# Masking the second halves' diagonal blocks after the exponential, on GpSimd, in a new order of stages

## The chip, the cores and the metric

The kernel runs on one core of a Trainium2 chip, in one launch. The metric is device microseconds of one execution, host transfers not included. Four engines compute: TensorE (PE in the profile; its weight loads are PEld), VectorE (DVE), ScalarE (ACT) and GpSimd (POOL). SyncE (SP) only issues DMAs. The engines run at the same time and meet in semaphores.

## The reference

One transformer layer on x of 2 batches x 1024 positions x 128 features, all in float32. First attention, then a mixture of experts:

```
x = x + attention(layernorm(x))      # 16 heads of 8 features, causal
x = x + experts(layernorm(x))        # 16 experts of width 64, the best 2 of a token; one shared expert

attention:  q, k, v = x Wq', x Wk', x Wv'
            q, k = layernorm per head, gamma and beta, then rotary embedding
            scores = q k' / sqrt(8); scores = where(key <= query, scores, -inf)
            out = softmax(scores) v; out Wo' + bo
experts:    top-2 routing over softmax(x gate_w') + gate_b, in 2 of 4 groups
            sum of combine * (silu(x We1 + be1) * (x We3 + be3)) We2 + be2, and the shared expert
```

The part that the change touches is the line with `where`. A key later than the query must end with probability zero.

## The kernel before

**Chunks and groups.** The 2 x 1024 positions are cut into four chunks of 512, x = 0 to 3. Chunk x is of batch x % 2 and half x // 2, so chunks 2 and 3 are the second halves. Heads go in four groups of four; a = 4 * x + group counts 16 of them, and a = 8 to 15 belong to the second halves. A second half attends to the 512 keys before it and to its own.

**Stages of one group.** `max` (PE, L672) multiplies queries by keys, and `maxred` (DVE, L1159) reduces each row to its maximum. `mneg` (POOL), `mturn` (PE), `mcopy` (ACT) and `mrow` (a DMA) put the negated maximum into two spare rows of the queries' operand. Then `scores` (PE, L695) gives scores with the maximum already subtracted, keys on the partitions. `exp` (ACT, L842) reads a pair of PSUM banks, 128x1024, and writes one of 8 buffers of `probs`. `pv` (PE, L718) multiplies those by the values into an accumulating bank. A burst s is what one `pv` takes: a group of a second half has seven, k = 0 to 3 over the older keys (two pairs of banks each), k = 4 and 5 with two pairs, k = 6 with one. The last three hold the eight 128x128 diagonal blocks, each for both heads of a pair: one block in a pair of banks of k = 4, two in a pair of k = 5 and in that of k = 6.

**The mask.** `mask_product` (L644) is a small bf16 matmul that adds -1e30 to the forbidden half of a block in PSUM: four for a block and pair of heads (two over 64 columns, two over 128). `max` does it for the diagonal units, before the reduction, and `scores` does it again for the diagonal blocks, before the exponential. Over the whole kernel that is 384 products in `max` and 512 in `scores`.

**Experts.** For each chunk and each of nine units (eight pairs of experts, one shared) `moeU` and `moeV` (PE, L766), `moe_t` and `moe_v` (ACT, L895 and L886), `moe_one` (POOL, L1077), `moe_a` (DVE, L1249), `moe_g` (POOL, L1084), `moe_h` (POOL, L496, times the combine weights, which `cstore` and `cload` bring through DRAM) and `moe_y` (PE, L782). The last chunk has no attention beside it and takes another way, with `moeG`, `moeL`, `wide` and less on POOL. `V_RING` is 4: `moe_v` of a unit waits for `moe_g` of the fourth before it. `cT` (PE, L744) turns the combine weights of a chunk.

**The order.** Every engine walks one list, `ORDER`, and executes those of its stages that stand in it, in that order; nothing overtakes on an engine. The number behind @ names the PSUM bank or banks. The list was written out by a planner beforehand.

Of the kernel before, what the change touches and what calls it, by code (L numbers as in the profile page):

```python
# [162 lines left out]
scores.16.1@01 max.8.5@23 exp.16.1 maxred.8.5 gate.0@6 gate_read.0 max.8.6@01 moeV.0.0@5 moeV.0.1@3 moe_v.0.0 maxred.8.6
gate_exp.0 route1.0 moe_v.0.1 moeV.0.2@6 moe_v.0.2 max.8.7@45 maxred.8.7 scores.17.0@01 exp.17.0 mrow.6 rope_join.3
qT.3@3 moeU.0.0@6 moeU.0.1@2 qT_lead.3 qT_rest.3 moe_t.0.0 moe_a.0.0 moe_t.0.1 scores.18.0@45 mrow.7 exp.18.0 max.8.8@01
moe_one.0.0 maxred.8.8 moe_one.0.1 qT_mid.3 moeU.0.2@3 moe_a.0.1 moe_t.0.2 moe_g.0.0 moeV.0.3@6 scores.18.1@01
scores.19.0@45 pv.16 pv.17 exp.18.1 exp.19.0 moe_one.0.2 scores.19.1@01 exp.19.1 scores.20.0@45 exp.20.0 moe_g.0.1
route2.0 moe_a.0.2 moeV.0.4@3 moe_v.0.3 route3.0 moeU.0.3@0 moe_t.0.3 moe_g.0.2 moeU.0.4@1 moe_v.0.4 oturn.2 moe_t.0.4
max.8.9@45 maxred.8.9 moeU.0.5@6 moe_a.0.3 moe_a.0.4 moe_t.0.5 moe_one.0.3 moe_g.0.3 moe_one.0.4 moeV.0.5@2 moe_v.0.5
pv.18 moe_a.0.5 moe_one.0.5 moe_g.0.4 max.8.10@45 max.8.11@01 maxred.8.10 maxred.8.11 scores.21.0@23 exp.21.0 cT.0@6  # L170
max.8.12@45 maxred.8.12 max.8.13@23 maxred.8.13 max.9.0@01 cT_read.0 cstore.0 mmin.8 moeV.0.6@6 moe_g.0.5 moe_v.0.6
pv.19 maxred.9.0 max.9.1@45 scores.21.1@23 exp.21.1 cload.0.0 moeV.0.7@6 moe_v.0.7 mneg.8 mturn.8@1 mcopy.8 mrow.8
max.9.2@23 maxred.9.1 scores.22.0@45 max.9.3@01 maxred.9.2 maxred.9.3 moe_h.0.1 cload.0.2 xbo.1 pv.20 scores.22.1@23
exp.22.0 exp.22.1 max.9.4@45 moeU.0.6@6 moe_t.0.6 max.9.5@23 maxred.9.4 maxred.9.5 moe_a.0.6 scores.23.0@01 pv.21
scores.24.0@23 scores.24.1@45 oT_read.2 exp.23.0 exp.24.0 moe_one.0.6 max.9.6@01 kT.3@6 pv.22 maxred.9.6 pv.23 kT_lead.3
kT_rest.3 oturn.3 max.9.7@01 oT_read.3 oback.1 exp.24.1 scores.25.0@45 exp.25.0 moe_h.0.2 moeU.0.7@3 moe_t.0.7
# [1217 lines left out]
```

## Time and profile before

| | |
|---|---|
| three runs | 378.99, 384.35, 385.32 us, median 384.35 |
| the profiled execution | 383.55 us, of it a span of 381.7 us |
| PE busy | 338.2 us, 89% of the span |
| DVE busy | 291.7 us, 76% |
| ACT busy | 233.5 us, 61% |
| POOL busy | 181.1 us, 47% |
| mean granted TensorE clock | 0.95 |

The span runs from the first to the last instruction of the profiled execution; the 1.85 us around it belong to its time. A chain is the path that ended last, followed back from the last instruction. A timeline row merges neighbours of one kind on one engine: the start, the length until the end of the last, and in brackets what the engine waited for. Matmuls overlap in the array, so the cost of one in such rows is the difference of two starts and not the length.

### The profile page before, as it was taken

How to read it: one execution, taken by the hardware profiler on the slowest of the kernel's cores; microseconds unless marked ns; L12 is line 12 of the kernel's file. 1: busy time of each engine (PE TensorE's matmuls, PEld its weight loads, DVE VectorE, ACT ScalarE, POOL GpSimd, SP SyncE). 2: the span in 40 equal slices, each digit the busy share in tenths (PEclk: the TensorE clock that was granted, in tenths of full speed). 3: DMA queues.
4: the chain of work that ended last, by engine and by line, in shares of the span. 5: the costliest groups of instructions: out<-in, count | busy, mean ns of one | idle time of the engine just before them, and what ended most of it. 6: DMA issues, size and time to landing. Idle time of an engine off the chain costs nothing.

```text
span 381.7 us, 7937 instructions
## 1 busy us (share of the span) xinstructions
PE 338.2 (89%) x2883; PEld 148.3 (39%) x2883; DVE 291.7 (76%) x508; ACT 233.5 (61%) x340; POOL 181.1 (47%) x304
## 2 busy tenths in 40 slices
PE   2667689899799898999999989999999999969995
PEld 1233345445444334353334332434334433434342
DVE  5693789899999999779998899987686830656742
ACT  1656129776759566774576767786676999424320
POOL 1587985998855438657504502034060028471000
PEclk9966559999999999999999999999999999988999
DMA  4997004103200036002043130001000019000000
GB/s 124 200 217 162 16 3 127 43 3 92 78 3 4 0 106 149 2 0 72 0 100 87 38 75 2 3 1 30 2 2 2 3 53 202 0 0 0 3 27 27
DMA packets 26840, 19.65 MB, mean 51 GB/s; under 512 B 9713, under 2 KB 23570, under 8 KB 26738
## 3 DMA queue, kind: packets, MB, share of 16 engines
q1 hardware_dynamic: 25410, 18.09, 20.8%
q10 hardware_dynamic: 1392, 1.05, 1.2%
q8 instruction: 24, 0.39, 0.5%
q14 instruction: 14, 0.11, 0.1%
HBM read 11.56 MB, written 1.15 MB: 33 GB/s over the span
## 4 chain that ended last, share of the span: by engine, by line
PE 61%; DVE 24%; issue 5%; ACT 5%; DMA 2%; POOL 1%; ACTq 1%; SPq 1%; DVEq 0%; POOLq 0%
PE psum L766 14%; PE psum L718 13%; PE psum L782 7%; PE psum L695 7%; PE psum L672 7%; DVE mx_diag L1159 7%; PE psum L644 5%; DVE mx_full L1159 4%; ACT probs L842 2%; PE psum L626 2%; DVE mv L1249 2%; PE psum L635 1%; PE psum L736 1%; PE psum L728 1%; DVE resid L1148 1%
## 5 line engine op out<-in xcount | busy, mean ns | idle before, releaser
L842 ACT ACTIVATE probs<-psum 128x1024 f32<-128x1024 f32 x144 | 142.3, 1024 | 49.7 <-PE psum L644 27.1
L1159 DVE TENSOR_REDUCE mx_diag<-psum 128x4 f32<-128x512 f32 (+2 forms) x96 | 96.0, 1041 | 23.3 <-PE psum L672 22.6
L1159 DVE TENSOR_REDUCE mx_full<-psum 128x2 f32<-128x1024 f32 x64 | 76.1, 1220 | 7.3 <-PE psum L672 7.0
L718 PE MATMUL psum<-probs,v_ones 128*18 128x512 f32 (+3 forms) x768 | 73.6, 489 | 0.2
L766 PE MATMUL psum<-x2T,w 128*128 128x512 f32 x144 | 71.8, 626 | 1.0 <-DVE mv L1249 0.9
L672 PE MATMUL psum<-k_st,q_st 62*128 62x512 bf16 (+3 forms) x384 | 60.6, 344 | 2.0 <-ACT probs L842 0.9
L644 PE MATMUL psum<-masks 64*128 64x128 bf16 (+2 forms) x896 | 51.5, 216 | 11.0 <-DVE mx_diag L1159 3.3
L695 PE MATMUL psum<-q_st,k_st 64*128 64x512 bf16 (+3 forms) x384 | 53.7, 328 | 3.1 <-DVE mv L1249 0.9
L644 PEld LDWEIGHTS psum<-masks 64*128 64x128 bf16 x896 | 33.6, 96 | 42.8 <-DVE mx_diag L1159 14.9
L1077 POOL TENSOR_SCALAR mh<-mh 128x512 f32<-128x512 f32 x27 | 16.8, 623 | 62.3 <-ACT mh L895 62.1
L1084 POOL TENSOR_TENSOR mh<-mh,mv 128x512 f32<-128x512 f32 x27 | 34.1, 1270 | 11.8 <-DVE mv L1249 11.8
L766 PEld LDWEIGHTS psum<-x2T,w 128*128 128x128 f32 x144 | 25.7, 195 | 29.5 <-issue 24.4
L782 PE MATMUL psum<-mh,w 128*128 128x512 f32 x72 | 37.1, 624 | 0.0
L496 POOL TENSOR_TENSOR mh<-mh,early 128x512 f32<-128x512 f32 x24 | 30.6, 1287 | 12.6 <-DMA early<-combine_scratch 12.4
L695 PEld LDWEIGHTS psum<-q_st,k_st 64*128 64x128 bf16 x384 | 17.4, 94 | 41.8 <-ACT probs L842 18.1
L672 PEld LDWEIGHTS psum<-k_st,q_st 62*128 62x128 bf16 x384 | 20.2, 100 | 22.3 <-ACT probs L842 9.7
L1249 DVE SCALAR_TENSOR_TENSOR mv<-psum,b,mv 128x512 f32<-128x512 f32 x27 | 19.6, 743 | 9.7 <-ACT mh L895 9.3
L718 PEld LDWEIGHTS psum<-probs,v_ones 128*18 128x18 f32 x768 | 16.7, 97 | 25.3 <-issue 22.8
L886 ACT ACTIVATE mv<-psum,b3h 128x512 f32<-128x512 f32 x27 | 18.4, 687 | 11.0 <-PE psum L766 10.6
L1033 POOL CAST negmax<-mx_diag 128x16 bf16<-128x16 f32 x16 | 3.2, 198 | 43.3 <-DVE mx_diag L1324 40.2
L895 ACT ACTIVATE mh<-psum,b1h 128x512 f32<-128x512 f32 x27 | 18.5, 688 | 6.5 <-PE psum L766 6.4
L635 PE MATMUL psum<-w_qkv,xnT 128*128 128x384 f32 x32 | 19.0, 750 | 2.8 <-ACT xnT L848 2.7
(162 smaller groups left out, 359.0 us busy)
## 6 DMA issues: line engine op xcount, KB each, us to landing
early<-combine_scratch SPq DMA_DIRECT2D x24, 256.0 KB, 4.8
q_st<-parts SPq DMA_DIRECT2D x24, 128.0 KB, 2.4
k_st<-parts SPq DMA_DIRECT2D x18, 128.0 KB, 2.4
w<-in_We SPq DMA_DIRECT2D x3, 512.0 KB
k_st<-in_c_pad SPq DMA_DIRECT2D x8, 128.0 KB, 6.3
out<-xs SPq DMA_DIRECT2D x4, 256.0 KB, 2.3
xs<-in_x SPq DMA_DIRECT2D x3, 256.0 KB, 5.9
k_st<-parts ACTq DMA_DIRECT2D x6, 128.0 KB, 4.0
```

What stands on the lines that cost most here:

```text
L496: engine.tensor_tensor(h, h, comb_b[:, u, :], ALU.mult).then_inc(weighted, 1)
L635: pe.matmul(w[:, 0:3 * P], xnT[:, t * P:(t + 1) * P], w_qkv[:, :], start=True, stop=True).then_inc(work_full, 1)
L644: return pe.matmul(dst, masks[r, slot, :], blocked, start=start, stop=stop, skip_group_check=True)
L672: last = pe.matmul(w[:, par, i * keys:(i + 1) * keys], q_st[r, x % 2, 2 * g + m, q0:q0 + P], k_st[r, b, 2 * g + m, k0:k0 + keys], start=(w ...
L695: last = pe.matmul(w[:, par, col:col + cols], k_st[rows(par), b, 2 * g + m, kt * P:(kt + 1) * P], q_st[rows(par), x % 2, 2 * g + m, q0:q0 ...
L718: last = pe.matmul(acc[32 * j:32 * j + 2 * VC, q0:q0 + cols], own_then_zeros, probs[:, n % P_RING, j % 2, col:col + cols], start=(kt == 0 ...
L766: pe.matmul(w, (w1 if kind in ("moeU", "moeG") else w3)[:, unit(n), :], x2T[:, x % 2, :], start=True, stop=True).then_inc(work_full, 1)
L782: last = pe.matmul(y, w2[:, unit(n), :], mh[:, at % T_RING, :], start=(n == 0), stop=(n == UNITS - 1), skip_group_check=True)
L842: act.activation(probs[:, n % P_RING, :, :], wpair("scores", (s, i)), ACT.Exp, scale=SCALE).then_inc(exp_done, 1)
L1084: pool.tensor_tensor(t, t, mv[:, at % V_RING, :], ALU.mult).then_inc(gate_done, 1)
L1159: dve.tensor_reduce(dst[:, a % 2, :, pairs[0]:pairs[0] + nm, qt], w, AX.X, ALU.max, negate=True).then_inc(max_free, 1)
L1249: dve.scalar_tensor_tensor(out=v, in0=wbank("moeU", (x, n)), scalar=b1[:, unit(n):unit(n) + 1], in1=v, op0=ALU.add, op1=ALU.mult).then_inc ...
```

## The change

`SELECTED` names chunks 2 and 3. For their diagonal blocks `scores` no longer issues mask products. The exponential is taken of the unmasked scores, and a new stage `mask` on GpSimd then writes zeros where the key is later than the query, in place in `probs`. `pv` of such a burst waits for it. Chunks 0 and 1, and the masks of all `max` stages, stay.

```diff
+SELECTED = (2, 3)
+MASK_LIST = [(s, i) for s, i in BANK_LIST if BURSTS[s][0] // NG in SELECTED and BURSTS[s][1] >= 4 * half_of(BURSTS[s][0] // NG)]
+MASKS = {key: n for n, key in enumerate(MASK_LIST)}
+MASKS_TO = {s: max(n for (q, _), n in MASKS.items() if q == s) + 1 for s, _ in MASK_LIST}
...
-                own = [col for m, kt, col, cols, q0 in pieces if kt >= 4 * c]
+                own = [col for m, kt, col, cols, q0 in pieces if kt >= 4 * c and x not in SELECTED]
...
+                if s in MASKS_TO:
+                    pe.wait_ge(masked, MASKS_TO[s])
                 pe.wait_ge(exp_done, BANKS_TO[s])
...
+            def causal(s, i):
+                a, k = BURSTS[s]
+                pieces = bursts_of(half_of(a // NG))[k][i]
+                pool.wait_ge(exp_done, BANKS[s, i] + 1)
+                p = probs[:, BANKS[s, i] % P_RING, :, :]
+                for _, _, col, _, _ in pieces:
+                    own = p[:, :, col:col + P]
+                    last = pool.affine_select(own, own, [[0, 2], [1, P]], ALU.is_ge, 0.0, base=0, channel_multiplier=-1)
+                last.then_inc(masked, 1)
```

There are 40 `mask` stages with 64 selections of 128 partitions x 256 elements. `ORDER` is replaced as a whole: the same 1316 stages in another order and with other banks, and the 40 new ones. Its start for ACT before and after:

```
before: qkv_read.7 norm_apply.2 qT_lead.0 kT_lead.0 qT_mid.0 xT_read.2 kT_mid.0 stack_act.0.1.0 stack_act.0.1.1 stack_act.0.1.2 qkv_read.8
after:  qkv_read.7 qT_lead.0 kT_lead.0 weights2_read.0 qT_mid.0 kT_mid.0 norm_apply.2 stack_act.0.1.1 xT_read.2 stack_act.0.1.2 stack_act.0.1.0 qkv_read.8
```

Its end, by engine (every stage of the engine from there to the first stages of the last chunk's experts):

```
PE before:   pv.75 scores.77.1 scores.78.0 moeU.2.5 scores.78.1 scores.79.0 pv.76 pv.77 pv.78 pv.79 moeV.2.6 moeV.2.7 moeV.2.8
             moeU.2.6 moeU.2.7 moeU.2.8 proj.3 moe_y.2.0 moe_y.2.1 moe_y.2.2 moe_y.2.3 x2T.3 moe_y.2.4 gate.3
PE after:    scores.77.1 cT.2 pv.75 pv.76 scores.78.0 scores.78.1 scores.79.0 moeV.2.4 moeU.2.4 moeU.2.5 moeV.2.5 pv.77 pv.78 pv.79
             moeV.2.6 moeV.2.7 moeV.2.8 proj.3 moeU.2.6 moeU.2.7 moe_y.2.0 moe_y.2.1 moeU.2.8 moe_y.2.2 moe_y.2.3 moe_y.2.4 x2T.3 moe_y.2.5 gate.3
POOL before: moe_h.2.1 moe_g.2.4 moe_h.2.2 moe_h.2.3 moe_h.2.4 moe_one.2.5 moe_one.2.6 moe_one.2.7 moe_one.2.8 moe_g.2.5 moe_g.2.6
POOL after:  mask.77.0 mask.77.1 moe_one.2.3 mask.78.0 mask.78.1 mask.79.0 moe_g.2.2 moe_g.2.3 moe_one.2.4 moe_one.2.5 moe_h.2.1 moe_h.2.2
             moe_g.2.4 moe_g.2.5 moe_h.2.3 moe_h.2.4 moe_h.2.5 moe_one.2.6 moe_g.2.6
ACT after:   exp.77.0 exp.77.1 cT_read.2 exp.78.0 exp.78.1 moe_v.2.4 moe_t.2.4 exp.79.0 moe_v.2.5 moe_t.2.5 moe_v.2.6 moe_v.2.7 moe_v.2.8 moe_t.2.6 moe_t.2.7 norm2_apply.3
DVE:         before oturn.7 moe_a.2.5 oT_read.7 oback.3, after oturn.7 oT_read.7 oback.3 moe_a.2.5
SP:          before store.1 cload.2.0 cload.2.2 cload.2.1 cload.2.3, after cload.2.1 cload.2.2 cload.2.0 cload.2.3 store.0 store.1
```

## Rows read from the trace of the kernel before

**Rows 1.** The page: busy time of each engine, and the chain that ended last.
```profile
PE 338.2 (89%) x2883; PEld 148.3 (39%) x2883; DVE 291.7 (76%) x508; ACT 233.5 (61%) x340; POOL 181.1 (47%) x304
...
PE 61%; DVE 24%; issue 5%; ACT 5%; DMA 2%; POOL 1%; ACTq 1%; SPq 1%; DVEq 0%; POOLq 0%
```

**Rows 2.** Windows: busy us (count) of PE, PEld, DVE, ACT, POOL; clock, DMA.
```profile
0.00:40.00 40.00, 21.12 (x49) 10.99 (x49) 23.62 (x84) 20.72 (x53) 24.28 (x65) 0.83 0.87 172
40.00:160.00 120.00, 107.87 (x1249) 52.77 (x1249) 109.63 (x154) 77.49 (x115) 86.26 (x146) 0.93 0.19 48
160.00:260.00 100.00, 94.96 (x865) 37.69 (x863) 89.81 (x119) 68.62 (x85) 36.10 (x44) 1.00 0.15 37
260.00:325.32 65.32, 65.20 (x592) 25.07 (x590) 38.23 (x72) 50.23 (x63) 22.71 (x39) 1.00 0.17 41
325.32:339.57 14.25, 11.00 (x34) 4.82 (x30) 10.52 (x29) 5.77 (x10) 6.52 (x8) 1.00 0.00 0
339.57:381.70 42.13, 38.02 (x102) 16.98 (x102) 19.86 (x53) 10.64 (x16) 5.26 (x5) 0.91 0.04 13
```

**Rows 3.** Timeline of PE: mask products between other stages, and one bank pair unmasked.
```profile
216.35 0.40 PE L672 MATMUL psum<-k_st,q_st 62*128 62x512 bf16 x2
216.68 1.05 PE L718 MATMUL psum<-probs,v_ones 128*18 128x512 f32 x8
...
220.46 0.26 PE L644 MATMUL psum<-masks 64*128 64x64 bf16 x4
220.54 0.40 PE L672 MATMUL psum<-k_st,q_st 62*128 62x512 bf16 x2
...
304.63 0.35 PE L644 MATMUL psum<-masks 64*128 64x64 bf16 x8
304.80 0.40 PE L695 MATMUL psum<-q_st,k_st 64*128 64x384 bf16 x4
```

**Rows 4.** Groups by line and shape on POOL: count | busy us, mean ns | idle before.
```profile
L1084 POOL TENSOR_TENSOR mh<-mh,mv 128x512 f32<-128x512 f32 x27 | 34.1, 1270 | 11.8 <-DVE mv L1249 11.8
L1077 POOL TENSOR_SCALAR mh<-mh 128x512 f32<-128x512 f32 x27 | 16.8, 623 | 62.3 <-ACT mh L895 62.1
L472 POOL TENSOR_TENSOR early<-early,hrstd 128x1024 f32<-128x1024 f32 x3 | 7.1, 2355 | 0.1
L1001 POOL TENSOR_SCALAR nr_pool<-nr_pool 128x128 f32<-128x128 f32 x9 | 2.7, 301 | 0.8
L1017 POOL TENSOR_SCALAR nr_pool<-nr_pool 128x4 f32<-128x4 f32 x18 | 4.6, 254 | 1.6
```

**Rows 5.** Timeline: one L1017 beside a DVE instruction that reads two operands from SBUF.
```profile
22.04 1.23 DVE L472 TENSOR_TENSOR early<-early,hrstd 128x1024 f32<-128x1024 f32 x1
22.15 1.17 POOL L1017 TENSOR_SCALAR nr_pool<-nr_pool 128x4 f32<-128x4 f32 x1
```

**Rows 6.** Timeline of ACT: the last nine exponentials, and what follows them.
```profile
315.51 8.37 ACT L842 ACTIVATE probs<-psum 128x1024 f32<-128x1024 f32 x9
323.74 0.72 ACT L895 ACTIVATE mh<-psum,b1h 128x512 f32<-128x512 f32 x1
```

**Rows 7.** Timeline of PE: the last pv stages and the stages up to gate.3.
```profile
321.92 0.33 PE L644 MATMUL psum<-masks 64*128 64x64 bf16 x8
322.19 3.21 PE L718 MATMUL psum<-probs,v_ones 128*18 128x512 f32 x40
325.32 5.42 PE L766 MATMUL psum<-x2T,w 128*128 128x512 f32 x12
330.58 1.05 PE L728 MATMUL psum<-w_o,o_normT 128*128 128x128 f32 x8
331.47 1.88 PE L782 MATMUL psum<-mh,w 128*128 128x512 f32 x4
333.28 1.12 PE L786 MATMUL psum<-combT,b 17*128 17x512 f32 x2
...
339.57 0.66 PE L626 MATMUL psum<-ident,w_raw 128*128 128x128 f32 x4 [3.26 <-ACT w_raw L923]
```

**Rows 8.** Timeline: combT's copy, the combine weights' loads, the first products with them.
```profile
310.69 0.56 ACT L955 COPY combT<-psum 16x512 f32<-16x512 f32 x1
...
312.85 5.26 SPq L582 DMA_DIRECT2D early<-combine_scratch  x8
...
322.28 2.53 POOL L496 TENSOR_TENSOR mh<-mh,early 128x512 f32<-128x512 f32 x2 [0.83 <-DMA early<-combine_scratch]
```

**Rows 9.** Timeline of ACT and DVE: norm2_apply.3, and the last step before it.
```profile
337.68 0.16 DVE L1127 SCALAR_TENSOR_TENSOR shift<-mean_var,rstd 128x4 f32<-128x4 f32 x1
...
337.88 1.65 ACT L923 ACTIVATE w_raw<-xs,shift,rstd 128x128 f32<-128x128 f32 x4 [6.41 <-DVE shift L1127]
```

**Rows 10.** Windows: the stretch around the last clock dip.
```profile
338.90:345.70 6.80, 6.13 (x17) 3.75 (x18) 2.00 (x11) 2.91 (x6) 5.93 (x5) 0.59 0.00 0
```

**Rows 11.** Timeline: a weight load's wait at 186 us; chunk 2's norm_apply on ACT.
```profile
186.50 0.10 PEld L695 LDWEIGHTS psum<-q_st,k_st 64*128 64x128 bf16 x2 [1.75 <-DVE mv L1249]
...
28.50 1.65 ACT L923 ACTIVATE early<-xs,shift,rstd 128x128 f32<-128x128 f32 x4 [1.67 <-DVE roped L487]
```

More of the change, by code:

```diff
@@ L163 @@
[L163 to L176, printed above, removed]
-moeV.0.8@2 cload.0.1 maxred.9.7 moe_v.0.8 proj.1@6 scores.25.1@45 exp.25.1 moe_a.0.7 max.9.8@01 maxred.9.8 proj_read.1
@@ new lines @@
+maxred.8.8 moe_g.0.1 moe_g.0.2 moeV.0.5@1 kT_lead.3 cT.0@2 kT_rest.3 max.8.9@45 moe_v.0.5 cT_read.0 moe_one.0.3
+maxred.8.9 max.8.10@01 maxred.8.10 scores.19.1@23 scores.20.0@45 cstore.0 cload.0.1 exp.19.1 exp.20.0 moe_a.0.3
+max.8.11@01 maxred.8.11 scores.21.0@23 exp.21.0 pv.17 max.8.12@45 oturn.2 qT_mid.3 scores.21.1@01 exp.21.1 qT_low.3
+maxred.8.12 max.8.13@23 maxred.8.13 mmin.8 mneg.8 moeU.0.4@6 moe_t.0.4 moeU.0.5@1 max.9.0@45 moe_t.0.5 oT_read.2
+moe_a.0.4 moe_g.0.3 cload.0.0 scores.22.0@23 moe_h.0.1 moe_h.0.2 exp.22.0 maxred.9.0 pv.18 pv.19 pv.20 moe_a.0.5
@@ new lines @@
+max.9.9@23 maxred.9.8 maxred.9.9 moe_t.0.7 moe_a.0.7 scores.26.0@45 exp.26.0 pv.24 moe_one.0.6 max.9.10@01 max.9.11@45
+scores.26.1@23 exp.26.1 moeU.0.8@6 moe_t.0.8 maxred.9.10 maxred.9.11 scores.27.0@01 exp.27.0 max.9.12@23 norm2_rstd.1
+norm2_apply.1 maxred.9.12 pv.25 scores.27.1@45 moe_a.0.8 max.9.13@01 maxred.9.13 mmin.9 exp.27.1 pv.26 x2T.1@6
+x2T_read.1 max.10.0@01 scores.28.0@23 scores.28.1@45 maxred.10.0 exp.28.0 gate.1@6 gate_read.1 moe_g.0.5 exp.28.1
+moe_h.0.3 max.10.1@23 max.10.2@01 mask.28.0 gate_exp.1 moe_y.0.0 moe_one.0.7 moe_one.0.8 moe_g.0.6 moe_g.0.7 maxred.10.1
@@ new lines @@
+maxred.10.2 route1.1 moeV.1.0@5 moe_v.1.0 mneg.9 moeU.1.0@4 moe_t.1.0 moe_a.1.0 moeV.1.1@0 moe_v.1.1 max.10.3@23
+maxred.10.3 moe_one.1.0 mturn.9@1 moe_h.0.4 mask.28.1 mcopy.9 mrow.9 pv.27 max.10.4@45 max.10.5@01 moe_y.0.1 maxred.10.4
+maxred.10.5 scores.29.0@23 exp.29.0 max.10.6@01 scores.29.1@45 exp.29.1 moe_y.0.2 moeU.1.1@3 moe_t.1.1 kT_low.3
+moeV.1.2@2 moe_v.1.2 moeV.1.3@4 moe_g.0.8 moe_g.1.0 route2.1 moe_a.1.1 maxred.10.6 moe_one.1.1 moe_g.1.1 moe_v.1.3
+mask.29.0 moe_h.0.5 route3.1 moe_y.0.3 scores.30.0@23 scores.31.0@01 exp.30.0 exp.31.0 moe_h.0.6 moeU.1.2@4 moe_y.0.4
@@ new lines @@
+scores.31.1@01 cload.0.3 exp.31.1 max.10.7@23 maxred.10.7 stack.3.1.2 moeU.1.3@5 moe_t.1.2 moe_t.1.3 moeU.1.4@0
+moe_a.1.2 moe_a.1.3 stack.3.1.1 stack.3.1.0 moe_one.1.2 moe_one.1.3 moe_g.1.2 moe_t.1.4 moeV.1.4@1 moe_v.1.4 moeV.1.5@2
+moe_v.1.5 cT.1@1 moe_h.0.7 cT_read.1 max.10.8@45 max.10.9@23 moe_a.1.4 scores.32.0@01 exp.32.0 moe_h.0.8 maxred.10.8
+pv.28 maxred.10.9 moe_one.1.4 max.10.10@45 maxred.10.10 scores.32.1@01 exp.32.1 max.10.11@23 maxred.10.11 moe_y.0.5
+mask.29.1 max.10.12@45 maxred.10.12 scores.33.0@01 max.10.13@23 exp.33.0 maxred.10.13 pv.29 mmin.10 scores.33.1@45
@@ new lines @@
+moeU.2.4@4 moeU.2.5@5 moe_t.2.4 mask.78.1 moe_a.2.4 exp.79.0 moeV.2.5@2 moe_v.2.5 cload.2.2 pv.77 pv.78 mask.79.0 pv.79
+moeV.2.6@1 moeV.2.7@3 moeV.2.8@4 oturn.7 oT_read.7 oback.3 moe_g.2.2 moe_t.2.5 proj.3@2 moe_a.2.5 moe_v.2.6 moe_g.2.3
+moe_v.2.7 moe_one.2.4 moe_one.2.5 moeU.2.6@5 moeU.2.7@1 cload.2.0 moe_h.2.1 moe_h.2.2 moe_g.2.4 moe_g.2.5 moe_h.2.3
+moe_v.2.8 moe_y.2.0 moe_y.2.1 proj_read.3 norm2.3 moe_t.2.6 moe_a.2.6 moe_h.2.4 moe_h.2.5 moe_t.2.7 moeU.2.8@0 moe_a.2.7
+moe_y.2.2 norm2_apply.3 moe_one.2.6 moe_g.2.6 moe_h.2.6 moe_y.2.3 moe_y.2.4 cload.2.3 x2T.3@4 x2T_read.3 moe_y.2.5
```

208 lines of the change are left out of this document (102 added, 106 removed).

## The prediction

> **What bounds the kernel.** I read the page first. PE is busy for 338.2 of 381.7 us, and the chain that ended last lies on it for 61%, on DVE for 24%, on ACT for 5% and on POOL for 1% [rows 1]. An average hides the stages, so I read windows next [rows 2]. The first 160 us belong to chunks 0 and 1: there DVE has 109.6 of 120 us and PE 107.9. From 160 to 260 us PE is busy for 95.0 of 100 and DVE for 89.8: both are near full. From 260 us to the end of attention at 325.32 PE has 65.2 of 65.3 us, ACT 50.2, DVE 38.2. Behind it lies a tail of one chunk's experts, on PE except for a wait of 3.26 us for the last layernorm [rows 7]. POOL, to which the change gives work, has 36.1 + 22.7 = 58.8 us in the 165.3 us of chunks 2 and 3. So the engine that is relieved is the one that bounds, and the one that is loaded has room.
>
> **The removed products.** A diagonal block costs four products. The difference of starts counts: four take 0.08 us (220.46 to 220.54), eight 0.17 us (304.63 to 304.80) [rows 3]. The two halves of the array's rows evidently work side by side, which is why the 0.26 and 0.35 us shown as lengths mislead. 64 blocks x 0.085 = **5.4 us** of PE, all of it after about 157 us. Where a float32 stage follows, eight products take 0.27 us (321.92 to 322.19), but an unmasked pair of banks also shows 0.33 us to its follower, some 0.12 above its neighbours' 0.21 [rows 3, 7]. The upper bound is 64 x 0.27 / 2 = 8.6 us, the lower bound 0, if PE then waits for DVE or ACT. I take 4.0 us. Some 25 blocks lie where PE alone is full (2.1 us, all of it kept), 39 where DVE is at 90% (3.3 us, of which I keep 1.9, a choice).
>
> **The selections.** The trace has none. The nearest rows are one-input POOL instructions: 0.30 us for 128 columns and 0.62 for 512 [rows 4], so 0.41 us for 256. I take 0.41, the row kind that it is nearest to. The bounds are 0.30 below and 2.36 above, the longest POOL row. 64 x 0.41 = 26 us go into the 106.5 us that POOL has free, and cost 0. That cover is gone from (165.3 - 58.8) / 64 = **1.66 us** each. The new wait is at `pv`: behind it on PE stand other stages, and exponentials of later banks wait for it, since `probs` has 8 buffers. In the order each diagonal `pv` has other PE stages between it and its exponential. It is bare only at the end: exp.79.0, two selections, pv.79. Before, the last exponential ended at 323.9 and attention at 325.3, 1.4 us later [rows 6, 7]. After, 0.8 for the selections and 0.43 for pv.79 (half of a full burst, whose columns it has half of: 0.86) fit in the same 1.4. Cost 0; at 1.27 us each it would be 1.6.
>
> A row and a rule speak against selections on GpSimd. L1017 takes 0.25 us on average, but 1.17 beside a DVE instruction with two SBUF inputs [rows 4, 5]. The Trainium skill (GPSIMD Engine Reference, Key points) says that GpSimd shares its SBUF interfaces with VectorE and contends with DVE instructions of two SBUF inputs; by that rule, and by that row, a selection would cost up to 1.17 us. In the stretch DVE mainly reduces PSUM, with one input, so I leave 0.41. The result that this would give is rival three.
>
> **The new order, start.** The same stages move. ACT's norm_apply.2, 1.65 us [rows 11], no longer stands between the rotary embedding and the copy of its result, which helps the first `max`. It now stands before chunk 0's key stacking DMAs, issued on the same queue, which gives it back. Bounds -3 to +3 us, because PE idles for 12.1 us between 40 and 160 and the new order can fill or widen that; I take 0.
>
> **The new order, end.** Call T the end of the last pv (325.32 before). Before, x2T.3 starts at T + 14.25: six U and V stages of 0.88 come ahead of proj.3 at T + 5.26, and from its start to that of x2T.3 it is 8.99 us [rows 7]. After, only three come ahead, so proj.3 starts at T + 2.6 and the layernorm could release x2T.3 at T + 11.6. Three things take most of that back.
> - The combine weights. cT.2 and its copy now stand behind exp.77.1. From there ACT has the copy (0.56), three exponentials (0.93) a V and a U stage (0.69 each) to T - 1.4, so the copy ends at T - 5.6. The loads start 1.6 us later, as before, at T - 4.0 [rows 8]. moe_h.2.1 needs part 0, which is now loaded third. The third part landed 9.4 us after the first issue (312.85 to 322.28), so it is here at T + 5.4.
> - POOL's queue. The last selection ends at T - 0.6. moe_g.2.2, 2.3 and two moe_one end at T + 3.2, then it waits to T + 5.4. moe_h.2.1, 2.2, moe_g.2.4, 2.5, moe_h.2.3 and 2.4, at 1.27 each, end at T + 6.7, 8.0, 9.2, 10.5, 11.8, 13.0.
> - ACT. moe_v.2.8 waits for moe_g.2.4 (a ring of four), then two tanh: T + 11.3. norm2_apply.3 takes 1.65 [rows 9], so x2T.3 is ready at T + 13.0.
>
> PE then has proj.3, two U and moe_y.2.0 to T + 6.2, waits 0.5 us for moe_h.2.1, has moe_y.2.1 with its bias, moeU.2.8 and moe_y.2.2 to T + 10.4, waits 1.4 us for moe_h.2.3, then 0.3 for moe_h.2.4. It ends moe_y.2.4 at T + 13.9. So x2T.3 starts 0.35 us earlier than before, with one more moe_y (0.9) ahead of it and not behind: **1.3 us** gained. The bounds are 3.5 (no wait) and -1 (loads 2.4 us later). The stages after x2T.3 are the same, PE carries them before, and I see no new wait. Stores 0 and 1 move behind the loads; SyncE is idle there.
>
> **The clock.** After the 3.26 us wait, with PE doing nothing, the clock granted in the 6.8 us from 338.9 is 0.59, that is mostly the lower level, 1.2 GHz [rows 7, 10]. At full clock that stretch does 0.41 x 6.8 = 2.8 us more. A 1.75 us wait at 186.5 us was not followed by a fall: the window there shows 1.00 [rows 2, 11]. The longest wait that I find in the new tail is 1.4 us, so I take the dip as gone: **2.8 us**.
>
> **The sum.** The profiled execution took 383.55 us (span 381.7 and 1.85 around it), 0.8 below the median of 384.35. 383.55 - 4.0 - 1.3 - 2.8 = **375.5 us**, 2.3% below the median.
>
> **Rivals.**
> 1. *The dip stays*, because the waits are longer than I worked out: 378.3 us. For it: two waits close together, and 0 to 3 us of uncertainty in the loads. Chance 0.17.
> 2. *The new order closes gaps too*: all 5.4 us, and 3 of the 12.1 + 5.2 us that PE idles from 40 to 325 us: 383.55 - 5.4 - 3 - 4.1 = 371 us. Chance 0.12.
> 3. *The last group's queue.* With 1.17 to 1.27 us a selection, eight take 9.4 to 10.2 us, while their five exponentials and what stands between them take 5 x 0.93 + 2 x 0.69 + 0.56 = 6.6. Attention ends 3 to 4 us later: 379 us. Chance 0.11.
> 4. *The products were hidden.* PE waits for DVE or ACT instead, and the 4.0 us are not there: 379.5 us. For it: DVE at 90% to 260 us, ACT at 50.2 of 65.3 afterwards. Against it: PE's 99.8% there. This is also the case where the change does nothing of what it is for. Chance 0.10.
> 5. *Slower: POOL becomes the bound of chunks 2 and 3.* It decides from 1.66 us a selection. At 2.0 us POOL needs 58.8 + 128 = 186.8 us where 165.3 are there, 21.5 more: about 383.6 + 21.5 - 1.3 = 404 us. For it: the operation compares positions, and only 2.36 us bounds it. Against it: four times the one-input price at its size. Slower than before by 2% begins at about 1.8 us. Chance 0.10, which includes 0.02 that it stays within 2%.
>
> **The numbers.** The forecast has 0.40, with 372 to 379 us as its own range. 2% is about what a measurement of this kernel can tell from no change; the border is at 376.7 us. Faster by more: 0.28 of the forecast, all 0.12 of rival 2, and 0.04, 0.02 and 0.02 of rivals 1, 3 and 4, where the start turns out well: 0.48. Slower: 0.08. Within 2%: 0.44. The range of 368.5 to 386 leaves out rival 5 and the best third of rival 2, some 0.15 in all.
>
> **What would show it.** L644 falls from 896 to 640 instructions. PE's busy time from 160 us to the end of attention falls by 4 to 6 us, and attention ends at about 321. The selections show 64 rows near 0.41 us; above 1.2, rival 3 shows as a wait of `pv` for POOL, and above 1.7, POOL is full. x2T.3 starts about 13.9 us after the last pv, with waits for moe_h.2.3 before it, and no clock below 1.0 behind it. If attention ends at 325 with PE idle for DVE or ACT, rival 4 holds. I am wrong altogether if the first 160 us move by more than 3 us either way.

## The result, and the profile after

The changed kernel takes **384.44 us** (median of 20 runs, 383.74 to 386.66). The kernel before has a median of 382.20 in as many runs (378.99 to 385.32), so the ratio is **1.0072, 95% interval 1.0047 to 1.0097**: 0.7% slower, where 2.3% faster was forecast. The profiled execution took 384.1 us, with a span of 382.4 us, 0.7 us more than before. The medians differ by 2.2 us. The rows below explain the 0.7. The other 1.5 us lie between executions: the profiled one of the kernel before took 383.55, which is 1.35 above its own median, and that of the kernel after is 0.3 below its own. The time of the kernel before goes with its mean granted clock: among its executions beside the experiments, 380.48 us had 0.964 and 385.36 us had 0.942.

The page of the kernel after: busy time of each engine, the chain that ended last, then two groups (line, engine, operation, operands, count | busy us, mean ns | idle before). They answer [rows 1] and [rows 4].

```profile
PE 333.5 (87%) x2627; PEld 139.4 (36%) x2627; DVE 301.2 (79%) x508; ACT 233.1 (61%) x340; POOL 201.5 (53%) x368
...
PE 64%; DVE 22%; ACT 5%; issue 3%; SPq 2%; DMA 2%; ACTq 0%; DVEq 0%
...
L1053 POOL TENSOR_SCALAR_AFFINE_SELECT probs<-probs 128x256 f32<-128x256 f32 x64 | 24.5, 406 | 60.9 <-ACT probs L852 60.7
...
L652 PE MATMUL psum<-masks 64*128 64x128 bf16 (+2 forms) x640 | 38.4, 214 | 8.4 <-DVE mx_diag L1181 6.1
```

PE is relieved by 4.7 us, 256 products are gone, and a selection costs 0.406 us. Yet the span did not shrink. DVE is busy for 9.5 us more, with the same 508 instructions: some of them have become longer. One sign that the prediction named is absent: PE's busy time from 160 us to the end of attention was to fall by 4 to 6 us, and it is 95.17 + 64.98 = 160.2 us, as before (94.96 + 65.20), because more of the work now stands behind 160 us.

Windows of the kernel after, columns as in [rows 2], cut at its own end of attention (T = 325.11) and at x2T.3:

```profile
0.00:40.00 40.00, 18.74 (x46) 11.02 (x47) 25.51 (x84) 17.19 (x42) 19.07 (x54) 0.78 0.81 163
40.00:160.00 120.00, 106.22 (x1218) 51.34 (x1216) 109.17 (x154) 78.57 (x123) 83.91 (x155) 0.95 0.20 49
160.00:260.00 100.00, 95.17 (x726) 33.62 (x724) 91.49 (x118) 70.03 (x87) 47.79 (x76) 1.00 0.16 39
260.00:325.11 65.11, 64.98 (x512) 22.68 (x510) 38.06 (x72) 51.34 (x64) 30.42 (x68) 1.00 0.04 9
325.11:342.74 17.63, 12.88 (x36) 4.87 (x33) 15.82 (x28) 4.86 (x9) 12.50 (x12) 1.00 0.54 123
342.74:382.40 39.66, 35.48 (x100) 15.84 (x100) 21.18 (x54) 11.08 (x17) 7.83 (x8) 0.93 0.04 14
```

Attention ends 0.2 us earlier than before, not 4. The stretch from T to x2T.3 is 17.63 us where it was 14.25, and DVE is busy for 15.82 of it (10.52 before). What follows x2T.3 is 2.5 us shorter.

**The start.** Timeline of DVE after: the rotary embedding of chunk 0.

```profile
22.85 1.23 DVE L480 TENSOR_TENSOR early<-early,hrstd 128x1024 f32<-128x1024 f32 x1
24.11 2.17 DVE L483 TENSOR_TENSOR early<-early,g_cos 128x1024 f32<-128x1024 f32 x1
26.21 2.35 DVE L486 TENSOR_TENSOR roped<-early,g_sin 128x512 f32<-128x512 f32 x2
```

Beside it, timeline of POOL:

```profile
23.07 4.33 POOL L1072 TENSOR_TENSOR xs<-xs,bo_b 128x512 f32<-128x512 f32 x2 [1.51 <-DMA bo_b<-in_bo]
```

The same DVE lines in the kernel before:

```profile
23.30 1.23 DVE L475 TENSOR_TENSOR early<-early,g_cos 128x1024 f32<-128x1024 f32 x1
24.44 1.29 DVE L478 TENSOR_TENSOR roped<-early,g_sin 128x512 f32<-128x512 f32 x2
```

The new order puts `xbo.0` and `xbo.1` (POOL adds the output bias to the residual, L1072) beside the first rotary embedding. DVE's 1.23 becomes 2.17 and its 1.29 becomes 2.35; POOL's two adds are longer too, 4.33 us together where the two later ones take 1.3 us each. The first `maxred` starts at 43.1 us where it was 40.8.

**The end.** Timeline of DVE after: the Newton steps of the last layernorm's reciprocal root, 128x4 elements each. The lines left out are alike (1.19 each, then 1.18, 0.54, 0.16).

```profile
331.36 0.17 DVE L1121 TENSOR_SCALAR seed<-rstd 128x4 int32<-128x4 int32 x1
331.57 1.14 DVE L1123 SCALAR_TENSOR_TENSOR nr<-seed 128x4 f32<-128x4 f32 x1
332.74 1.19 DVE L1124 TENSOR_TENSOR nr<-nr,rstd 128x4 f32<-128x4 f32 x1
333.96 1.19 DVE L1125 SCALAR_TENSOR_TENSOR seed<-nr,seed 128x4 f32<-128x4 f32 x1
...
340.84 0.16 DVE L1149 SCALAR_TENSOR_TENSOR shift<-mean_var,rstd 128x4 f32<-128x4 f32 x1
```

POOL beside them:

```profile
331.43 2.48 POOL L504 TENSOR_TENSOR mh<-mh,early 128x512 f32<-128x512 f32 x2 [3.90 <-DMA early<-combine_scratch]
333.87 2.49 POOL L1106 TENSOR_TENSOR mh<-mh,mv 128x512 f32<-128x512 f32 x2
336.32 3.70 POOL L504 TENSOR_TENSOR mh<-mh,early 128x512 f32<-128x512 f32 x3
```

And PE, in answer to [rows 7]:

```profile
332.74 1.13 PE L792 MATMUL psum<-mh,w 128*128 128x512 f32 x2 [1.09 <-POOL mh L504]
...
337.63 2.35 PE L792 MATMUL psum<-mh,w 128*128 128x512 f32 x4 [0.80 <-POOL mh L504]
342.74 1.00 PE L634 MATMUL psum<-ident,w_raw 128*128 128x128 f32 x4 [2.76 <-ACT w_raw L933]
```

The same steps in the kernel before, on DVE and then on POOL:

```profile
333.72 0.93 DVE L1119 TENSOR_SCALAR rstd<-mean_var 128x4 f32<-128x4 f32 x1
334.68 1.19 DVE L1099 TENSOR_SCALAR seed<-rstd 128x4 int32<-128x4 int32 x1
335.91 0.16 DVE L1101 SCALAR_TENSOR_TENSOR nr<-seed 128x4 f32<-128x4 f32 x1
```

```profile
334.58 1.26 POOL L496 TENSOR_TENSOR mh<-mh,early 128x512 f32<-128x512 f32 x1
338.66 1.27 POOL L1084 TENSOR_TENSOR mh<-mh,mv 128x512 f32<-128x512 f32 x1 [2.81 <-DVE mv L1249]
```

Nine steps of 0.16 us and `shift` ran before while POOL, from 335.84 to 338.66, waited for DVE. After, POOL has seven products of 1.24 us back to back there, and seven DVE steps take 1.14 to 1.19 us, about one POOL product each. That is 7 x 1.02 + 0.38 = 7.5 us in front of `norm2_apply.3`. Two other terms go against it. The two steps ahead of the nine, `rstd` and `seed`, were already held in the kernel before (0.93 and 1.19 us) and take 0.17 us each now, 1.8 us less. And proj.3 starts 2.4 us earlier relative to T (T + 2.8, where T + 2.6 was forecast). 7.5 - 1.8 - 2.4 = 3.3, and `shift` does come 3.4 us later behind T: 15.7 us where it was 12.4.

### The profile page after: what moved, and what is told of

It is laid out like the page before. It is cut to its first block, busy times and chain, and to the rows that moved or that the text cites. A ratio compares the mean times of both kernels' runs of the same rounds, so it can differ in the third digit from the quotient of the medians.

```text
span 382.4 us, 7508 instructions
## 1 busy us (share of the span) xinstructions
PE 333.5 (87%) x2627; PEld 139.4 (36%) x2627; DVE 301.2 (79%) x508; ACT 233.1 (61%) x340; POOL 201.5 (53%) x368
## 4 chain that ended last, share of the span: by engine, by line
PE 64%; DVE 22%; ACT 5%; issue 3%; SPq 2%; DMA 2%; ACTq 0%; DVEq 0%
PE psum L728 16%; PE psum L776 12%; PE psum L703 9%; PE psum L680 8%; PE psum L792 7%; PE psum L652 5%; DVE mx_diag L1181 4%; DVE mx_full L1181 4%; PE psum L634 3%; ACT probs L852 3%; PE psum L643 2%; DMA xs<-in_x 2%; DVE nr L1123 1%; DVE mv L1271 1%; DVE nr L1124 1%
## 5 line engine op out<-in xcount | busy, mean ns | idle before, releaser
L728 PE MATMUL psum<-probs,v_ones 128*18 128x512 f32 (+3 forms) x768 | 76.4, 495 | 0.0
L776 PE MATMUL psum<-x2T,w 128*128 128x512 f32 x144 | 71.0, 615 | 3.5 <-DVE mv L1271 2.0
L680 PE MATMUL psum<-k_st,q_st 62*128 62x512 bf16 (+3 forms) x384 | 57.6, 333 | 1.9 <-DVE mv L1271 1.1
L1053 POOL TENSOR_SCALAR_AFFINE_SELECT probs<-probs 128x256 f32<-128x256 f32 x64 | 24.5, 406 | 60.9 <-ACT probs L852 60.7
L652 PE MATMUL psum<-masks 64*128 64x128 bf16 (+2 forms) x640 | 38.4, 214 | 8.4 <-DVE mx_diag L1181 6.1
L792 PE MATMUL psum<-mh,w 128*128 128x512 f32 x72 | 38.3, 632 | 2.0 <-POOL mh L504 1.9
L652 PEld LDWEIGHTS psum<-masks 64*128 64x128 bf16 x640 | 23.9, 95 | 37.1 <-DVE mx_diag L1181 15.8
L776 PEld LDWEIGHTS psum<-x2T,w 128*128 128x128 f32 x144 | 24.4, 189 | 32.6 <-issue 19.2
L680 PEld LDWEIGHTS psum<-k_st,q_st 62*128 62x128 bf16 x384 | 19.1, 95 | 23.7 <-DVE mx_full L1181 7.6
L728 PEld LDWEIGHTS psum<-probs,v_ones 128*18 128x18 f32 x768 | 15.6, 97 | 26.9 <-issue 24.0
L1099 POOL TENSOR_SCALAR mh<-mh 128x512 f32<-128x512 f32 x27 | 17.0, 635 | 11.8 <-ACT mh L905 11.8
```

The source lines that it names most:

```text
L652: return pe.matmul(dst, masks[r, slot, :], blocked, start=start, stop=stop, skip_group_check=True)
L680: last = pe.matmul(w[:, par, i * keys:(i + 1) * keys], q_st[r, x % 2, 2 * g + m, q0:q0 + P], k_st[r, b, 2 * g + m, k0:k0 + keys], start=(w ...
L728: last = pe.matmul(acc[32 * j:32 * j + 2 * VC, q0:q0 + cols], own_then_zeros, probs[:, n % P_RING, j % 2, col:col + cols], start=(kt == 0 ...
L776: pe.matmul(w, (w1 if kind in ("moeU", "moeG") else w3)[:, unit(n), :], x2T[:, x % 2, :], start=True, stop=True).then_inc(work_full, 1)
L792: last = pe.matmul(y, w2[:, unit(n), :], mh[:, at % T_RING, :], start=(n == 0), stop=(n == UNITS - 1), skip_group_check=True)
L1053: last = pool.affine_select(own, own, [[0, 2], [1, P]], ALU.is_ge, 0.0, base=0, channel_multiplier=-1)
```

## The experiments

Theory S (sharing): a DVE instruction with two SBUF operands waits for the POOL instruction that runs, and the new order puts POOL's products beside such chains, at the start and at the end. Its rivals were that the selections are what costs, and that the order is slower for other reasons (late combine weights above all). All were timed in five rounds. The ratio is always to the kernel before. Times inside an execution come from one profile each, and their first exponentials lie up to 0.6 us apart between kernels whose order up to there is the same, so differences of that size say nothing.

**Only the selections, in the order of before.**

```diff
 ORDER = the list of before, with each mask stage added:
-... exp.28.0 ...
+... exp.28.0 mask.28.0 ...
```

> The selections alone: the sequence of before, each selection stage right behind its exponential. Theory S (the removed products are worth 3 to 5 us of PE between 138 and 297 us, and the new sequence gives them back by putting GpSimd work beside small VectorE instructions): 378 to 380 us, with the last pv at 321 to 323 us instead of 325.3. Rival R (the products were hidden, or the wait of pv for GpSimd eats them): 381.5 to 384 us.

Measured: 404.36 us, ratio 1.0565 (1.0505 to 1.0624). Both expectations missed. Timeline of POOL in it:

```profile
207.66 0.41 POOL L1056 TENSOR_SCALAR_AFFINE_SELECT probs<-probs 128x256 f32<-128x256 f32 x1 [11.37 <-ACT probs L855]
208.02 0.20 POOL L1046 CAST negmax<-mx_diag 128x16 bf16<-128x16 f32 x1
```

The selection is as cheap as elsewhere. But it waits at the head of POOL's queue for its exponential, and behind it stands the `mneg` of a later group. DVE had finished its input at 204.12 us (L1349), so it is held up for 3.9 us. The wait of 11.37 us is 28 times the selection's length. The total of such waits says little: it is 72.6 us here and 60.7 in the changed kernel, so what counts is which stage stands behind them. Up to exp.28.0, the first exponential with a selection behind it, the trace keeps step with the kernel before (156.79 us, 156.85 before). exp.31.1 starts 7.2 us late, which is ahead of the wait shown, exp.38.0 11.2 us late, which is behind it, and attention ends 23.9 us late. PE stands idle more, and the clock is part of the loss: granted 0.90 from 150 to 200 us and 0.95 from 215 to 349, where the kernel before has 1.00. How the 23.9 us divide among single waits is not shown. That 404 us is also the time of my rival of a slow selection is chance: the mechanism is another.

**Only the new order, products still on PE.**

```diff
-SELECTED = (2, 3)
+SELECTED = ()
 ORDER = the new list without the 40 mask stages
```

> The new sequence alone: mask products of chunks 2 and 3 back on PE, no selections. Theory S: the sequence alone costs 5 to 6 us against before, 386 to 389 us, 3 to 5 us more than the changed kernel. Rival R: within 1 us of the changed kernel, 383.5 to 385.5 us.

Measured: 387.02 us, 1.0104 (1.0055 to 1.0153). The order alone costs about 1%. Attention ends at 328.12, 2.8 us later than before. With the changed kernel's 325.11, the exchange of products for selections gains 3.0 us there, of which 0.3 are there before exp.28.0 (163.06 us, 162.73 in the changed kernel), where no product is removed yet.

**`xbo` late.** The two stages go behind exp.7.1 and exp.12.0, and nothing else is changed.

```diff
-qT_rest.0 xbo.0 xbo.1 kT_rest.0
+qT_rest.0 kT_rest.0   (xbo.0 behind exp.7.1, xbo.1 behind exp.12.0)
```

> The changed kernel, with the two additions of the output bias (xbo.0, xbo.1 on GpSimd) no longer beside the rotary embedding of chunk 0 on VectorE but behind exp.7.1 and exp.12.0. Theory S: the two VectorE products there take 1.23 and 1.29 us again instead of 2.17 and 2.35, the first maximum starts at 41 us instead of 43.1, and the time falls by 1.5 to 2.5 us to 382 to 383 us. Rival Q (the first maximum waits for the key stacking DMAs, which now stand behind norm_apply.2 on ACT): no change, 384 to 385 us.

Measured: 382.83 us, 0.9992 (0.9960 to 1.0025). Timeline of DVE in it, the same steps as above:

```profile
23.86 1.23 DVE L485 TENSOR_TENSOR early<-early,g_cos 128x1024 f32<-128x1024 f32 x1
25.00 1.28 DVE L488 TENSOR_TENSOR roped<-early,g_sin 128x512 f32<-128x512 f32 x2
```

Both lengths are back, the first `maxred` starts at 41.2, the first exponential at 55.06 (57.10 in the changed kernel), and attention ends at 323.10: both 2.0 us earlier. S holds at the start. The medians differ by 1.6 us. In the profiled execution the span is only 0.3 us shorter, since it took 1.7 us more behind the end of attention, with a granted clock of 0.67 from 340 to 346 us.

**POOL waits for the layernorm.** `moe_g.2.4` goes ahead, and the first product with combine weights waits for the last norm.

```diff
+            if (x, n) == (NX - 2, 1):
+                engine.wait_ge(last_norm, 1)
```

> The changed kernel, with GpSimd held before moe_h.2.1 until VectorE has finished the last layernorm's small instructions (moe_g.2.4 is moved ahead of moe_h.2.1, so that moe_v.2.8 is not held). Theory S: the nine small VectorE instructions take 0.16 us each again instead of 1.1 to 1.2, x2T.3 starts 12 to 14 us after the last pv instead of 17.6, and the time falls by 3 to 5 us to 379.5 to 381.5 us. Rival L (moe_y.2.3 and 2.4, late because the combine weights land late, hold x2T.3): no gain or a loss, since GpSimd starts those products 2 us later: 384 to 386 us.

Measured: 384.45 us, 1.0048 (1.0014 to 1.0081), an interval that overlaps the changed kernel's. Timeline of DVE in it, and then of POOL and PE:

```profile
330.41 0.17 DVE L1145 TENSOR_SCALAR rstd<-mean_var 128x4 f32<-128x4 f32 x1
330.61 0.17 DVE L1125 TENSOR_SCALAR seed<-rstd 128x4 int32<-128x4 int32 x1
...
331.21 0.16 DVE L1129 SCALAR_TENSOR_TENSOR seed<-nr,seed 128x4 f32<-128x4 f32 x1
...
332.58 0.16 DVE L1153 SCALAR_TENSOR_TENSOR shift<-mean_var,rstd 128x4 f32<-128x4 f32 x1
```

```profile
332.91 2.49 POOL L508 TENSOR_TENSOR mh<-mh,early 128x512 f32<-128x512 f32 x2 [4.90 <-DVE shift L1153]
```

```profile
334.24 1.13 PE L796 MATMUL psum<-mh,w 128*128 128x512 f32 x2 [3.34 <-POOL mh L508]
335.29 2.07 PE L800 MATMUL psum<-combT,b 17*128 17x512 f32 x2
...
343.19 0.60 PE L638 MATMUL psum<-ident,w_raw 128*128 128x128 f32 x4
```

The window behind that wait:

```profile
335.20:342.10 6.90, 6.90 (x9) 2.68 (x9) 0.00 (x0) 0.00 (x0) 6.82 (x7) 0.51 0.00 0
```

All nine steps are back at 0.16 and `shift` comes 8.2 us after T (324.36 here), not 15.7. Still x2T.3 starts at T + 18.8, later than in the changed kernel (T + 17.6), and no longer because of the norm: it doesn't wait for it. On PE five `moe_y` stand ahead of it. The second now waits 3.34 us for POOL, whose first product with combine weights starts at T + 8.6 where it was T + 6.3, and behind that wait the granted clock is 0.51 for 6.9 us: the bias pair, 1.12 us in the kernel after, takes 2.07. S is right about DVE's lengths, the rival about the time. But the edit took one limit away and made the other worse, so it doesn't show what the norm's delay costs by itself. In the changed kernel PE was done with those `moe_y` at T + 14.9 (342.74 less its wait of 2.76), so with POOL left as it was, 2.8 us is the most that a norm in time could give there.

**Both limits taken away.** `xbo` late; cT.2 behind pv.70, so that the combine weights land before T; `moe_g.2.4` and `.5` ahead of `moe_h`, which from `moe_h.2.2` waits for the norm; moeU.2.8 ahead of the first `moe_y`; x2T.3 ahead of three `moe_y`.

```diff
-pv.70 ... exp.77.1 cT.2 cT_read.2 cstore.2 ... moe_y.2.2 moe_y.2.3 moe_y.2.4 x2T.3 moe_y.2.5 gate.3
+pv.70 cT.2 ... exp.74.1 cT_read.2 cstore.2 cload.2.0 cload.2.2 cload.2.1 cload.2.3 ... x2T.3 moe_y.2.2 gate.3 moe_y.2.3 moe_y.2.4
+            if (x, n) == (NX - 2, 2):
+                engine.wait_ge(last_norm, 1)
```

> The changed kernel with both places mended: xbo.0 and xbo.1 late; cT.2 behind pv.70 with its copy, store and the loads (part 0 first) behind exp.74.1; on GpSimd moe_g.2.4 and 2.5 ahead of moe_h.2.1 and a wait for the last layernorm before moe_h.2.2; on PE moeU.2.8 before moe_y.2.0, x2T.3 ahead of moe_y.2.2, and moe_y.2.3 to 2.5 behind gate.3 and moeG.3.1. Theory S (start, combine loads and the contention in the layernorm are what the new sequence gave away): x2T.3 starts 10 to 11 us after the last pv instead of 17.6, no clock dip behind it, 375 to 379 us. Rival (the experts' stages behind bound the tail anyway): 381.5 to 383 us, as with xbo alone.

Measured: **377.85 us**, 0.9870 (0.9822 to 0.9918), faster than both kernels. Windows from T to x2T.3 and to the end, and the timeline of x2T.3:

```profile
325.19:335.24 10.05, 9.24 (x30) 4.07 (x27) 8.25 (x28) 5.08 (x9) 7.64 (x8) 1.00 0.04 11
335.24:377.80 42.56, 36.81 (x106) 15.67 (x106) 25.61 (x54) 10.97 (x17) 12.66 (x12) 0.98 0.04 13
```

```profile
335.24 0.66 PE L638 MATMUL psum<-ident,w_raw 128*128 128x128 f32 x4 [0.81 <-ACT w_raw L937]
```

x2T.3 starts 10.05 us after T, 7.6 earlier than in the changed kernel. PE waits 0.81 us for it, and the clock behind it is 0.98 (0.93 and, before the change, 0.91). What follows is 2.9 us longer, since three `moe_y` went there. Attention itself ended no earlier than in the changed kernel (T = 325.19), although `xbo` was moved. The profiled execution was the slowest of the six (379.66 us), and its trace shows where. Its first exponential starts at 55.04, as in the kernel with only `xbo` late (55.06). exp.18.0 starts 0.5 us later than there (116.63 and 116.08) and exp.21.1 1.9 us (136.07 and 134.13), and so it stays to the end. Window between those two, for that kernel and for this one:

```profile
116.08:136.07 19.99, 16.41 (x145) 7.34 (x140) 18.43 (x38) 12.71 (x18) 7.56 (x9) 0.91 0.17 41
116.08:136.07 19.99, 16.41 (x148) 7.85 (x144) 17.14 (x37) 11.74 (x17) 6.94 (x8) 0.83 0.07 15
```

So the lead of `xbo` was lost where less clock was granted, 0.08 x 20 = 1.6 us of it.

**The disputed cost put into the kernel before.** Five POOL products of two SBUF tiles, whose results nothing uses, behind `moe_h.2.5`.

```diff
+                elif kind == "noise":
+                    link(pool.tensor_tensor(noise[:, :], w1[...], w3[...], ALU.mult))
```

> The kernel before, with five products of two SBUF tiles (128x512 float32, results not used) added on GpSimd behind moe_h.2.5, so that GpSimd works while VectorE does the last layernorm's small instructions. Theory S (contention): those of them that have two SBUF inputs take 1.1 to 1.2 us instead of 0.16, one for each GpSimd product, x2T.3 starts 4 to 5 us later, and the time is 386 to 388 us. Rival (only the places in the new sequence matter, not the neighbourhood of the two engines): small instructions stay at 0.16 us, time 382 to 384 us.

Measured: 388.60 us, 1.0153 (1.0100 to 1.0206). Timelines of POOL, DVE and PE in it:

```profile
335.85 6.63 POOL L1078 TENSOR_TENSOR noise<-w 128x512 f32<-128x512 f32 x5
```

```profile
335.95 1.18 DVE L1108 SCALAR_TENSOR_TENSOR nr<-seed 128x4 f32<-128x4 f32 x1
337.16 0.16 DVE L1109 TENSOR_TENSOR nr<-nr,rstd 128x4 f32<-128x4 f32 x1
337.36 1.11 DVE L1110 SCALAR_TENSOR_TENSOR seed<-nr,seed 128x4 f32<-128x4 f32 x1
```

```profile
344.43 1.11 PE L629 MATMUL psum<-ident,w_raw 128*128 128x128 f32 x4 [8.07 <-ACT w_raw L926]
```

Five products, and exactly five of the nine DVE steps become 1.11 to 1.18 us long. 5 x 0.96 = 4.8 us, and x2T.3 starts 4.9 us later [rows 7]. What follows is 1.1 us longer, with a clock of 0.89 where it was 0.91. The mechanism is shown by itself, with its size.

**No mask on either engine.** The new order; chunks 2 and 3 get neither products before the exponential nor selections behind it, so their diagonal blocks are left unmasked.

```diff
-SELECTED = (2, 3)
+SELECTED = ()
-                own = [... if kt >= 4 * c and x not in SELECTED]
+                own = [... if kt >= 4 * c and x < B]
-                    pe.wait_ge(masked, MASKS_TO[s])
```

> The new sequence with the causal mask of chunks 2 and 3's diagonal blocks left out of the scores altogether: neither mask products nor selections. Theory S (selections cost next to nothing where the new sequence puts them): 383.5 to 384.5 us, at most 1 us less than the changed kernel. Rival (GpSimd's queue or the wait of pv takes part of the products' gain): 380 to 382.5 us.

Measured: 381.73 us, 0.9978 (0.9945 to 1.0012), 2.7 us below the changed kernel. I had expected 1 us at most. Attention ends at 323.20: the products are worth 328.12 - 323.20 = 4.9 us, and the selections cost 325.11 - 323.20 = 1.9 us of it. All kernels issue the exponentials in one order, so their starts tell where a difference arises:

| start of | before | new order, products | no mask | changed |
|---|---|---|---|---|
| exp.0.0 | 54.52 | 56.98 | 56.94 | 57.10 |
| exp.28.0 | 156.85 | 163.06 | 162.60 | 162.73 |
| exp.32.0 | 186.93 | 187.79 | 187.05 | 188.97 |
| exp.79.0 | 322.83 | 324.82 | 319.93 | 321.84 |

No product is removed before exp.28.0, so 0.5 of the 4.9 us is not theirs: 4.4 is. The selections' cost is 0.1 at exp.28.0 and 1.9 at exp.32.0 and stays so: it arises around the first of them, up to 189 us, and no later one adds to it. In the tail x2T.3 starts at 339.17, 16.0 us behind T and not 17.6: POOL's products begin 1.0 us behind the start of DVE's chain and not 0.3, so more of the short steps escape.

**The selections at a second place in the old order.** A burst's selections stand together, just ahead of the `pv` of the burst before it or right behind the burst's last exponential.

```diff
 ORDER = the list of before, with the mask stages added in 24 places:
-... maxred.9.11 pv.27 ...
+... maxred.9.11 mask.28.0 mask.28.1 pv.27 ...
```

> The sequence of before with the selections once more, now those of a burst together just before the pv of the burst before it (or right behind the burst's last exponential), not each behind its exponential. Theory S (the 404 us came from selections standing on GpSimd's queue ahead of mneg and moe stages and waiting there for an exponential): 379 to 384 us. Rival (the sequence of before has no room for the detour over GpSimd, wherever it stands): over 390 us.

Measured: 387.06 us, 1.0116 (1.0055 to 1.0178). Neither expectation held it. `mneg` is no longer held up, but `pv` waits for POOL (5.7 + 3.6 us in six waits). So selections couldn't be added to the old list at either of the two places tried. In the new order they are cheap, and it brings its own costs.

**The mended order with products on PE, no selections.**

```diff
-SELECTED = (2, 3)
+SELECTED = ()
```

> The mended kernel with the mask products of chunks 2 and 3 back on PE and no selections. If the removal of the products is worth what the pair with and without it in the unmended sequence showed (2.6 us), 380 to 381.5 us. If the selections only pay because of where GpSimd stood, no difference: 377.5 to 379 us.

Measured: 379.77 us, 0.9914 (0.9886 to 0.9942), against 0.9870 with selections. The time lies between the two expectations. The intervals overlap, and the two were not compared side by side: that the exchange gains 0.4%, some 1.9 us by the medians, is likely and not shown by the times. The profiles speak for it: from exp.28.0 to the end of attention it takes 164.9 us with products (160.54 to 325.47) and 162.5 with selections (162.68 to 325.19), 2.4 us less. In the new order as it was, the same stretch is 165.1 and 162.4.

**The kernel before with only its tail mended.** Old order and products. proj.3 goes behind moeV.2.8, oturn and oback ahead of `moe_a.2.5`, `moe_a.2.6` behind the norm's statistics, and POOL waits for the norm before `moe_g.2.5`.

```diff
-moeV.2.8 moeU.2.6 moeU.2.7 moeU.2.8 proj.3
+moeV.2.8 proj.3 moeU.2.6 moeU.2.7 moeU.2.8
+                    if (x, n) == (NX - 2, 5):
+                        pool.wait_ge(last_norm, 1)
```

> The kernel before, products and sequence kept, only its tail mended in the same way: proj.3 behind moeV.2.8, moe_a.2.5 and 2.6 off VectorE's way to the layernorm, GpSimd held before moe_g.2.5 until the layernorm's small instructions are done. Theory S: x2T.3 starts 10 to 11 us after the last pv instead of 14.25, no dip of the clock behind it, 377.5 to 380 us, so a large part of the mended kernel's gain has nothing to do with the selections. Rival (PE bounds the tail anyway): 382.5 to 384 us.

Measured: 380.00 us, 0.9939 (0.9906 to 0.9972). Timeline of PE in it:

```profile
325.35 2.84 PE L768 MATMUL psum<-x2T,w 128*128 128x512 f32 x6
...
336.18 0.60 PE L628 MATMUL psum<-ident,w_raw 128*128 128x128 f32 x4
```

10.8 us from T, no wait, without one selection. So about half of what the best version gains (0.6 of 1.3%) was to be had in the old kernel.

## Why the prediction was wrong

| step, as the prediction put it | predicted us | measured us | from |
|---|---|---|---|
| the removed products | -4.0 | -4.9 | end of attention, new order with products to no mask |
| the selections, in attention | 0 | +1.9 | no mask to changed kernel |
| the new order, start (`xbo`) | 0 | +2.0 | changed kernel to `xbo` late |
| the new order, rest of attention | 0 | +0.8 | what is left of 2.8 |
| the new order, from T to x2T.3 | -0.4 | +3.4 | 17.63 against 14.25 |
| behind x2T.3: one `moe_y`, clock | -3.7 | -2.5 | 39.66 against 42.13 |
| sum | -8.1 | +0.7 | spans 381.7 and 382.4 |

The measured 384.44 lies inside my range of 368.5 to 386, but that is luck: none of the five rivals describes it, and the direction was wrong. One sign of being wrong altogether did come true: the first 160 us moved by more than 3 us, with exp.28.0 starting 5.9 us later. The new order then goes through the rest of attention faster, even with the products (161.8 us from exp.28.0 to exp.79.0, where it was 166.0), so that 2.8 us of loss are left at its end.

- **The removed products** were right, on the safe side: 4.9 us in the table, 4.4 behind exp.28.0, of a possible 5.4. PE had been the bound, and rival 4 (they were hidden) is out.
- **The selections** had their price right (0.406 for a forecast 0.41), which ends rivals 3 and 5 as written. "They cost 0" failed. The 1.9 us arise between exp.28.0 and exp.32.0; PE's weight loads waited 1.4 us for a selection in the whole kernel, and the rest of the path I have not followed. What I priced was capacity, 26 us into 106 free ones. The first experiment shows that this price misses the queue: an engine that can't overtake holds up what stands behind a waiting selection. With selections of the same length and the same room the kernel loses 21 us, and about 4 with them at another place in the same order.
- **The new order, start** failed in its cause: +2.0 us lies inside my bounds (-3 to +3), but nothing in my text leads to it. I had followed ACT's norm_apply and the key stacks, and hadn't looked at what POOL would do beside DVE's widest instructions.
- **The new order, end** is the step that failed most: "norm2_apply.3 takes 1.65 [rows 9], so x2T.3 is ready at T + 13.0"; it was ready at T + 17.6. The 1.65 was right; the DVE chain ahead of it was not. The 8.99 us from the start of proj.3 to that of x2T.3 [rows 7] came out as 14.80. I had taken it from a profile in which POOL was idle beside the nine short steps, and in the same section moved POOL's products onto it. The queues had been worked out well: the loads started at T - 3.4 (forecast -4.0), proj.3 at T + 2.8 (2.6), `moe_h.2.1` at T + 6.3 (5.4). What wasn't worked out again were durations. x2T.3 was forecast for T + 13.9 and came at T + 17.6: 2.8 us of the difference are PE's wait for the norm, and the other 1.0 is that PE reached its place at T + 14.9, mainly since `moe_h.2.1` started 0.9 us later than forecast. The row that tells it stood in my own list: an L1017 of 0.25 us takes 1.17 beside a DVE instruction with two SBUF inputs [rows 5]. I used it for the selections alone, and dismissed it because DVE "mainly reduces PSUM"; I never turned it around. The same trace has it in this very chain, in `rstd` and `seed` at 0.93 and 1.19 us. The Trainium skill says it both ways (SBUF — State Buffer, Who interferes with whom): the shared pair of ports is held for a whole instruction, and a DVE instruction with two SBUF inputs contends with a GpSimd one that reads SBUF. The trace agrees: 0.16 us becomes 1.19 beside products of 1.24.
- **The clock** was half right. I had expected no wait there above 1.4 us. The wait ahead of x2T.3 shrank only from 3.26 to 2.76 us, and the dip behind it stayed, but became shorter. Window around it, of the kernel after:

```profile
342.60:346.00 3.40, 3.26 (x11) 2.17 (x11) 0.00 (x0) 1.26 (x3) 3.24 (x4) 0.54 0.00 0
```

It has 0.54 over 3.4 us, where [rows 10] had 0.59 over 6.8: 0.46 x 3.4 = 1.56 us lost and not 2.8. Behind a wait of 0.81 us (the mended kernel) and behind none (the last experiment) there was no dip.

The mechanism, fewer products on the bounding engine, was as forecast. It paid 3.0 us net of the selections (4.9 - 1.9). The order that came with it cost 2.8 in attention and 0.9 in the tail.

## What to carry to other kernels

When stages move, work out not only what each queue waits for but what now runs beside what: a DVE chain and a POOL stream that both read SBUF don't add up as if alone, and a chain of tiny instructions suffers most, since each can wait for a whole POOL instruction. In an engine that can't overtake, price an added instruction by the wait that it may hold at the head of the queue, not by its own length. And before you credit an edit, mend the old kernel's same spot too: here about half of the gain of the best version did not need the edit.
